# A stage's first layer norm moved into the stage before it, and combine weights spread over the partitions by DMA

## The reference

```python
def _layernorm(x, axis=-1, eps=1e-05):
    m = jnp.mean(x, axis=axis, keepdims=True)
    v = jnp.var(x, axis=axis, keepdims=True)
    return (x - m) / jnp.sqrt(v + eps)

x = x + mamba(_layernorm(x))             # state space block, 512 inner channels
x = x + ffn0(_layernorm(x))              # 8 experts, 2 of them per token, and a shared part
x = x + rotary(_layernorm(x))            # 16 heads of 16
x = x + ffn0(_layernorm(x))
x = x + (pattern and latent)(_layernorm(x))   # two attentions, mixed by a gate
x = x + ffn1(_layernorm(x))              # 16 experts of 176, 4 per token, shared part of 704 with a gate
x = x + grouped(_layernorm(x))           # 32 query heads on 8 key heads, and a linear memory
x = x + ffn1(_layernorm(x))
```

## Time and profile before

| | us |
|---|---|
| three runs, median (lowest to highest) | 4378.23 (4376.72 to 4392.27) |
| the profiled execution | 4388.44 |
| its span, first to last instruction | 4386.7 |
| PE busy | 3812.8 (87%) |
| DVE busy | 2547.1 (58%) |
| ACT busy | 1716.1 (39%) |
| POOL busy | 1356.8 (31%) |

### The profile page before, as it was taken

The page is one execution under the profiler, slowest core; times in us unless marked ns, Lnnn a source line. Parts: engine busy times, 40 slices in busy tenths (PEclk is TensorE's granted clock), DMA queues, the critical chain, the costliest instruction groups (busy, mean ns, idle before and its releaser), DMA issues. The chain is left out here.

```text
span 4386.7 us, 45573 instructions
## 1 busy us (share of the span) xinstructions
PE 3812.8 (87%) x16352; PEld 2470.1 (56%) x16352; DVE 2547.1 (58%) x4291; ACT 1716.1 (39%) x2934; POOL 1356.8 (31%) x1074
## 2 busy tenths in 40 slices
PE   5879888887988886999998988999888888889999
PEld 3657644445754443555555546788744444367887
DVE  5655456664456665767676756433466776564333
ACT  2423255653235552333333323222256656532222
POOL 3224312213321104333333324444322221144442
PEclk8989989998989987999999998999989999989999
DMA  2000000001000002000010111000000000010000
GB/s 75 1 22 21 14 1 1 1 1 43 17 6 6 5 22 77 25 20 25 19 26 17 27 34 38 26 26 19 19 1 1 1 1 1 6 42 22 26 9 20
DMA packets 32909, 83.35 MB, mean 19 GB/s; under 512 B 6320, under 2 KB 7472, under 8 KB 32304
## 3 DMA queue, kind: packets, MB, share of 16 engines
q1 hardware_dynamic: 32688, 80.44, 6.1%
HBM read 59.44 MB, written 4.19 MB: 15 GB/s over the span
## 5 line engine op out<-in xcount | busy, mean ns | idle before, releaser
L1175 DVE TENSOR_REDUCE max_cols<-ps 128x1 fp32r<-128x512 f32 x1024 | 634.7, 681 | 219.6 <-PE ps L1105 218.7
L1150 ACT ACTIVATE probs<-ps 128x512 f32<-128x512 f32 x1024 | 549.9, 606 | 262.1 <-PE ps L1114 173.4
L768 POOL TENSOR_TENSOR h_lo<-h,h_hi 128x512 fp32r<-128x512 f32 x304 | 392.1, 1290 | 819.2 <-ACT h_hi L853 819.2
L932 DVE TENSOR_TENSOR gated<-silu,ps 128x512 f32<-128x512 f32 x288 | 198.1, 688 | 680.6 <-PE ps L235 656.5
L847 ACT ACTIVATE silu<-ps 128x512 f32<-128x512 f32 x304 | 181.6, 598 | 896.8 <-PE ps L235 896.7
L233 PE MATMUL ps<-xn_hi,w_hi 128*128 128x512 f32 x1216 | 483.1, 397 | 0.0
L234 PE MATMUL ps<-xn_lo,w_hi 128*128 128x512 f32 x1216 | 476.9, 392 | 0.0
L235 PE MATMUL ps<-xn_hi,w_lo 128*128 128x512 f32 x1216 | 476.3, 392 | 0.0
L338 POOL CAST o_hi<-o_scaled 128x512 fp32r<-128x512 f32 x64 | 39.0, 610 | 869.2 <-DVE o_scaled L1197 869.2
L1120 PE MATMUL ps<-probs,v_aug 128*32 128x512 f32 x2048 | 294.9, 650 | 0.5 <-ACT probs L1150 0.5
L1105 PE MATMUL ps<-k_alone,q_stack 128*128 128x512 f32 x512 | 215.4, 444 | 53.8 <-DVE max_cols L1175 24.9
(11 more groups left out here) (462 smaller groups left out, 7842.7 us busy)
## 6 DMA issues: line engine op xcount, KB each, us to landing
raw<-in_w_ffn SPq DMA_DIRECT2D x76, 448.0 KB, 3.2
raw<-raw SPq DMA_DIRECT2D x256, 64.0 KB, 2.0
composed_inputs<-in_m_latent SPq DMA_DIRECT2D x2, 2560.0 KB, 9.4
raw<-in_w_mamba SPq DMA_DIRECT2D x8, 448.0 KB, 5.8
raw<-in_w_latent SPq DMA_DIRECT2D x5, 448.0 KB, 6.3
x<-in_x SPq DMA_DIRECT2D x4, 512.0 KB, 6.7
gated_pattern<-gated SPq DMA_DIRECT2D x4, 512.0 KB, 3.4
raw<-gated_pattern SPq DMA_DIRECT2D x4, 512.0 KB, 4.4
```

What stands on the lines that cost most here:

```text
L768: nc.gpsimd.tensor_tensor(HL[:, b % 3, :], hb[:, b % 2, :], HH[:, b % 3, :].bitcast(F32), ALU.subtract).then_inc(G.sem, G.step((s, ev)))
L932: nc.vector.tensor_tensor(ga if routed(i) else hb[:, i % 2, :], sg[:, i % 2, :], bank[2 + i % 2], ALU.mult).then_inc(V.sem, V.step((s, "ga ...
L1150: nc.scalar.activation(self.PB[:, n % 8, :], self.scores(n), ACT.Exp, scale=self.scale).then_inc(A.sem, A.step((s, ("exp", n))))
L1175: nc.vector.tensor_reduce(self.MB[:, self.tile_of(g, h) % 2, q, col:col + 1], self.psum(ev), op=ALU.max, axis=AX.X, negate=True).then_inc( ...
```

## The change

The helper functions take a follower (the name of the next stage) and use buffers that all stages share. Each stage puts the six events of a further batch, number NB = 4, into its list, in the places where its own later batches have them (before rotary only the first four, since rotary has steps of its own after them). That batch is batch 0 of x, read when the stage is done with it, and its marks are entered under the next stage's name. Every stage but the first begins without the six events (`begun`). In a feed-forward stage they stand four to six tiles behind the point at which the last group is done for batch 0; in mamba they stand in batches 2 and 3, in the others in the last batch's first group (latent: its pairs 3 to 5). Where `vec_clear` and `vec_begin` stood behind those events they are moved: to the head of the stage in pattern and grouped (in grouped `vec_begin` behind the first ("qk", 0, 0)), and behind "xn" of batch 0 in rotary. ffn cuts all pieces of group 0 first, latent all its pieces.

In ffn1 the "weights" matmul stays in group 0 only. In groups 1 to 3 the combine weights are spread by DMA: behind "turned" ACT copies the 17 rows to SBUF and stores them to DRAM, and behind "hi" of tile i ACT issues the load for tile i + 3, one DMA for each expert in the tile (one or two), each reading a row of 512 weights once for each partition.

```diff
+        xc, sq = sb("xc", [P, KD, L]), sb("sq", [P, KD, L])
+        XNH, XNL = sb("xn_hi", [P, KD, L], F32R), sb("xn_lo", [P, KD, L], F32R)
+        ln_roots = sb("ln_roots", [P, 1, L // 32])
...
+        FRONT = ("mean", "squared", "var", "dev", "xn", "xn cut")
+
+        def handed_on(follower):
+            return () if follower is None else FRONT[:4] if follower == "rotary" else FRONT
+
+        def hand_on(count, s, ev):
+            if ev[1] == NB:
+                count.mark((s + 1, (ev[0], 0)))
+
+        def x_of(b, k):
+            return x[:, k, b % NB * L:(b % NB + 1) * L]
+
+        def front_pe(pe, s, ev, psum, done):
             kind, b = ev[:2]
+            if kind == "mean" and b == NB and done is not None:
+                pe.wait_ge(V.sem, V.at((s, done)))
...
# ffn
-            begin = [(kind, 0) for kinds in chain[:3] for kind in kinds] + [("logits", 0), ("exp", 0)]
+            begin = ([] if begun else [(kind, 0) for kind in FRONT]) + [("logits", 0), ("exp", 0)]
...
+            first_done = (NG - 1) * NB * gt + gt - 1
+            for n, kind in enumerate(handed_on(follower)):
+                before[first_done + 4 + n // 2].append((kind, NB))
...
+            def by_matmul(i):
+                return routed(i) and (j == 0 or seq[i][0] == 0)
...
-                piece(0)
+                for t in range(gt if begun else 1):
+                    piece(t)
...
-                        if routed(i):
+                        if by_matmul(i):
                             if g == 0 and t == 0:
                                 pe.wait_ge(V.sem, V.at((s, ("turned", ch))))
...
# ffn, ACT
+                    elif kind == "turned" and j:
+                        act.wait_ge(V.sem, V.at((s, ev)))
...
+                        nc.scalar.activation(RW[64:64 + NE, :], ROUTE[64:64 + NE, :], ACT.Copy).then_inc(A.sem, A.step((s, ev)))
+                        act.wait_ge(A.sem, A.at((s, ev)))
+                        act.dma_start(combine_rows[0:NE, b * L:(b + 1) * L], RW[64:64 + NE, :]).then_inc(rows_kept, 16)
...
+                        n = i + NSPREAD
+                        if n < N and by_dma(n):
+                            act.wait_ge(rows_kept, 16 * rows_stored[0])
+                            ch = seq[n][1]
+                            for e, p0, p1 in experts_of(n):
+                                act.dma_start(SPREAD[p0:p1, n % NSPREAD, :], combine_rows[e:e + 1, ch * L:(ch + 1) * L].to_broadcast([p1 - p0, L])
+                                              ).then_inc(spread_in[n % NSPREAD], 16)
...
# ffn, DVE
+                        elif by_dma(i):
+                            after_last()
+                            dve.wait_ge(spread_in[i % NSPREAD], table[(s, "spread", i)])
+                            nc.vector.tensor_tensor(hb[:, i % 2, :], ga, SPREAD[:, i % NSPREAD, :], ALU.mult).then_inc(V.sem, V.step())
...
# rotary, pattern, grouped
+            for pos, kind in zip((2, 3, 5, 6, 9, 10), handed_on(follower)):
+                heads.put(NB - 1, 0, pos, (kind, NB))
...
# rotary, DVE
-                        if ev == ("mean", 0):
-                            heads.vec_clear(dve, s)
...
                         if b == 0:
+                            heads.vec_clear(dve, s)
                             begin()
...
# latent, POOL
-                cut_pieces(pool, d1[:ahead(s)], first[s])
+                cut_pieces(pool, d1[:npieces if begun else ahead(s)], first[s])
...
-        stages = [makers[name]() for name in plan]
+        stages = [makers[name](plan[s + 1] if s + 1 < len(plan) else None, s > 0) for s, name in enumerate(plan)]
```

More of the change, by code:

```diff
@@ L378, in mamba @@
                     events += [("xn", b + 1), ("xn cut", b + 1)]
+                else:
+                    events += [(kind, NB) for kind in handed_on(follower)[4:]]
                 events.append(("steps", b))
@@ L388, in mamba @@
                 events += [("scan", b, 1), ("y cut", b, 1)]
-                events += [("mean", b + 2), ("squared", b + 2)] if far else []
+                events += [(kind, b + 2) for kind in (front if far else handed_on(follower) if b + 2 == NB else ())[0:2]]
                 events += [("B", b, 2), ("step", b, 2), ("C", b, 2)]
@@ L1511, in pattern @@
             OH, OL, G4 = heads.OH, heads.OL, heads.G4
-            front = ("mean", "squared", "var", "dev", "xn", "xn cut")
             gate = ("gate", "gate exp", "gate spread")
             for b in range(1, NB):
-                for pos, kind in zip((2, 3, 5, 6, 9, 10), front):
+                for pos, kind in zip((2, 3, 5, 6, 9, 10), FRONT):
                     heads.put(b - 1, 0, pos, (kind, b))
@@ L1526, in pattern @@
                 heads.put(b + 1, 1, 2, ("out", b, 1))
-            begin = [(kind, 0) for kind in front] + [("qk", 0, i) for i in (0, 2, 1, 3)] + [("v", 0, q) for q in range(QT)]
+            begin = ([] if begun else [(kind, 0) for kind in FRONT]) + [("qk", 0, i) for i in (0, 2, 1, 3)] + [("v", 0, q) for q in range(QT)]
             begin += [(kind, 0) for kind in gate]
@@ L1779, in latent @@
                     put(g + 7, 0, ("tokens", b + 1))
-            events = [("mean", 0), ("squared", 0), ("var", 0), ("dev", 0), ("xn", 0), ("xn cut", 0)]
+            events = [] if begun else [(kind, 0) for kind in FRONT]
             events += [("mid", 0, m) for m in range(3)] + [("mid squared", 0), ("kp", 0), ("composed", 0), ("composed", 1),
@@ L1943, in pe @@
                     last = None
-                    if kind == "mean":
-                        for k in range(KD):
-                            last = nc.tensor.matmul(bank[slot(ev)], c256[:, :], x[:, k, ev[1] * L:(ev[1] + 1) * L],
-                                                    start=k == 0, stop=k == KD - 1)
-                    elif kind == "var":
-                        for k in range(KD):
-                            last = nc.tensor.matmul(bank[slot(ev)], c256[:, :], sq[:, k, :], start=k == 0, stop=k == KD - 1)
+                    if kind in ("mean", "var"):
+                        last = front_pe(pe, s, ev, bank[slot(ev)], ("tail", 0))
                     elif kind == "mid":
@@ L2311, in grouped @@
             heads.put(0, 2, 9, *a1[2])
-            begin = [(kind, 0) for kind in front] + [("qk", 0, 2)] + a0[0] + [("v", 0, q) for q in range(QT)]
+            begin = ([] if begun else [(kind, 0) for kind in FRONT]) + [("qk", 0, 2)] + a0[0] + [("v", 0, q) for q in range(QT)]
             heads.schedule(begin, [("out", NB - 1, 1)],
```

212 lines of the change are left out of this document (109 added, 103 removed).

## The result

The changed kernel takes 4339.34 us (median of 4 runs, 4337.85 to 4340.29), the kernel before 4385.25 in the same session (4 runs, 4376.72 to 4395.7): a ratio of 0.9896, with a 95% interval of 0.9878 to 0.9914. It is 46 us faster where 66 were forecast; the time lies inside the forecast's range (4288 to 4346), 27 us above its point of 4312, of which 7 us are the kernel before, 4385 here and 4378 in the three runs that the forecast started from. The time alone proves little: it lies nearer to the rivals R1 (4341) and R4 (4346) than to the forecast's point. What tells them apart is the time of each stage. Between the two profiled executions the spans differ by 50.0 us (4386.7 and 4336.7), and of these 50 the traces tell where each comes from. So the question of this part is why 16 us of the 66 are missing there.

The account below looks back on a forecast made before the run. TensorE was taken to bound the kernel, full in stretches and idle at starts. Starts 58.9 less 29.7 paid by stages before, plus 37.0 from combine weights, gave 66.2 us off 4378.2: 4312, range 4288 to 4346.

Parts of the forecast that it names:

- R1: Stage starts: replacement steps come later than seen or cost the stage before as much; only 37 us stays, 4341; chance 0.12.
- R4: Wide-stage tiles: second multiply comes 1.8 us late beside GpSimd's cut, losing 34 us of the combine-weights gain, 4346; chance 0.05.
- starts, narrow, two: Narrow feed-forward starts: logits wait only for the constants, 2.2 instead of 10.26 us; 8.1 each, 16.2 us gained.
- starts, wide, two: Wide feed-forward starts: logits wait only for the constants, 2.2 instead of 13.14 us; 10.9 each, 21.9 us gained.
- start, pattern: Pattern's start: the first product waits only for the third weight piece's cut; 7.3 us gained.
- start, grouped: Grouped's start: first product 10.6 us earlier, but the moved lone-keys memset delays what needs it; 9 us gained.
- start, latent: Latent's start: GpSimd's cuts end about 1695.4, so the squares that began at 1702.41 come earlier; 7.0 us gained.
- start, rotary: Rotary's start: only 0.6 us to be had, and clearing v_aug moves before the first heads; 2.5 us lost.
- stages before, all: Stages ahead of each start now run the moved mean and variance steps; 29.7 us paid in all.
- combine weights by DMA: Wide stages, groups 1 to 3: 168 matmuls fewer save 38.0 us, less 1 us for extra copies; 37.0 us gained.
- R2: Moved steps fill idle PE and shorter gaps keep the clock at 1.00; 84 us gained, 4294; chance 0.10.
- R3: Wide stages: the spread's DMA loads land late and hold PE; slower than before, 4462; chance 0.05.

Follow-up runs that it names:

- The reordered run: The changed kernel with latent's composed products before the key products, grouped's memset split, rotary's v_aug clearing at the stage's head: 4319.15 us, ratio 0.9859 to the kernel before.

## Why the prediction was right or wrong

| term | forecast | measured |
|---|---|---|
| starts, narrow, two | 16.2 | 15.1 |
| starts, wide, two | 21.9 | 26.3 |
| start, pattern | 7.3 | 7.3 |
| start, grouped | 9 | 6.1 |
| start, latent | 7.0 | 0.3 |
| start, rotary | -2.5 | -2.9 |
| stages before, all | -29.7 | -33.6 |
| combine weights by DMA | 37.0 | 31.3 |
| sum | 66.2 | 49.9 |

The narrow starts are read at the fourth x add of their stage, where the head start has settled; the wide ones at the first, so that the rest of group 0 stands under the combine weights.

**Feed-forward starts: right in the mechanism, in part by luck in the numbers.** The logits come 2.2 us after the start of narrow 1, and they come 8.1 us earlier in its stage than before, 11.0 in both wide ones: what the forecast says. It did not ask what comes behind the logits. There PE waits for the router's steps on VectorE, and these run beside POOL's cuts, whose collision the prediction knew from the earlier trace rows and looked for in the 84 tiles alone. At the first matmul with combine weights wide 1 had 9.3 us left and wide 2 had 13.1, at the first x add 10.8 and 15.5. So wide 1's 10.8 beside the forecast's 10.9 is luck, and what wide 2 gained beyond it is mostly a shorter collision and not rival R2's clock. The two narrow starts, 8.3 and 6.9, part at the same place: that matmul stands 17.3 us after the last write in one and 20.6 in the other.

**Pattern and rotary: right.** In rotary the wait for POOL's last cut ends 12.9 us after the last write in both kernels (534.34 - 521.47, and the 532.79 - 519.92 of the earlier trace rows):

```profile
534.34 0.25 DVE L1523 RECIPROCAL some<-roots 128x16 f32<-128x16 f32 x1 [10.36 <-POOL spare L236]
```

That wait gave nothing, and the memset behind it cost the 2.9 us. The reordered run takes it back.

**Latent: the step failed.** "The squares that follow on that engine began at 1702.41: 7.0 us" followed POOL and ended there. The squares did come 7.5 us earlier. What reads them is in PE's queue behind 32 composed products, and those were made slower by the very gap that the change left in front of them, 6.92 us for 3.68. They were already the last to end before: the squares of the earlier trace rows ended at 1704.30 and their sums began at 1706.44, behind the composed products. So the squares were not what the start waited for. After the change its chain is POOL's sixth cut (ended at 1692.15), the key products, the composed products and then the sums; and "what is late next", which the prediction asks at every other start, was not asked of PE's queue here.

**Grouped: the step was mis-sized.** The memset "delays what needs it by some of that": I took 1.6 us and at most 3.6, it was 4.5. The first product did come 10.4 us earlier, against the 10.6 of the forecast.

**Stages before: mis-sized by 3.9.** Narrow 3.8 each, wide 4.7 (33.3 against 28.6), where 3.5 stood. In the narrow stages the chunk with the moved steps takes 24.6 against 21.1, which is the 3.5; the other 0.3 is in the kernel with the spread alone too, which moves no steps, so it belongs to the shared xn tiles. Latent 7.1 for 5.5, grouped 5.1 for 4.6, pattern 2.7 for 0.3, mamba 6.0 for 4.2; rotary 0.4 for 4.6. Pattern, mamba and rotary have the clock in them: in rotary the last batch is 5.1 us longer (75.6 against 70.5 from the last copy of o_sums before it to its own last), near the 4.6, and the groups ahead of it 4.0 shorter with the same work; mamba's last output products ran at the lower level (0.43 us apart) nearly to the end.

**Combine weights by DMA: right alone, 5.7 short together.** 36.8 us in groups 1 to 3 of the kernel that has only this. In the changed kernel the shared xn tiles take back 2.0 a stage, which no step of mine had, and from its first to its fourth x add group 0 of wide 1 is 1.3 us longer (115.5 against 114.2). The change alone does not fix it: in nine of the other ten kernels that hand all on or all but rotary's it took 112.1 to 112.5. The spread landed in 1.7 to 4.9 us, under the 8.9 of cover, and no multiply waited for it; an issue on ACT took 0.34 us (median; 1.67 at most). R3 fell. So did R4, as it was put, for the tiles: the lock of the earlier trace rows is there and PE does not see it in groups 1 to 3.

**R1, starts swallowed,** was true of one start of eight in full (6.7 us) and of a second in part (2.9). With the shared xn tiles (4.0) that makes 13.6 of the missing 16. The stages before add 3.9, the rest of the combine weights 1.7 and the narrow and rotary starts 1.5; the wide starts take 4.4 off. So the near hit of the sum owes something to wide 2.

## What to carry to other kernels

When a step is taken out ahead of a stall, follow the chain to the engine that sets the pace and read its whole queue: an operand that is ready earlier gains nothing while another instruction is in front of the one that reads it. Memsets and constant set-up are part of a stage's start as much as its arithmetic; put them where their engine is idle in the new order, and split a long one. A collision of two engines that a full stream hides can cost its full length at a stage's start, where the engine that sets the pace waits for one of them: look for it there too. With identical instructions a stage of this kernel varied by 10 us together with its granted clock, so judge edits of a few us by the stage that they touch, and by more than one run of it.

## What the runs showed that I had not expected

- Reading the same values from another SBUF tile made 18 matmuls take 4.18 us instead of 4.08, in every version that has the shared xn tiles and in none without; three positions, two spacings of the halves and three distances of high and low did not change it by more than 0.03 us.
- A VectorE multiply of two SBUF tiles and GpSimd's cast lengthen each other (0.69 to 0.89 or 1.33 us, 0.94 to 1.41), and a stream in which the next step comes 1.7 us later (an estimate of the prediction, from the earlier trace rows) loses nothing by it. At the start of wide 1 the router's products of 64 elements took up to 1.85 us instead of 0.23, and PE waited 10.4 us for them and what follows them, against 7.2 in wide 2.
- The same pattern stage took 412.5, 419.0 or 422 to 423 us, clustered, and not spread over the range, at mean granted clocks of 0.91, 0.89 and 0.88.
